# Decay arguments of a state-space mixer: from TensorE sums of bf16 parts to ScalarE sums of broadcast float32

## The chip, the cores and the metric

One core of a Trainium2 chip runs the whole program. The metric is the device time of one execution in microseconds, from the runs of the kernel and from one profiled execution. A difference of about 0.2% (4 us) is what a measurement of this kernel can tell from no change.

## The reference, cut to what matters

Four blocks follow one another on x of 2 x 512 x 512: a block-sparse linear layer, an int4 feed-forward layer, the mixer, and the same feed-forward layer again. Only the mixer changes. For each of 128 heads (H, 64 wide) and each chunk of 128 tokens:

```python
A_dt = A[None, None, :] * dt                  # A = -exp(A_log), dt = softplus(...)
A_cumsum = jnp.cumsum(Ac, axis=-1)            # within a chunk of 128 tokens
Lmat = jnp.exp(segment_sum(Ac))               # exp(cum[l] - cum[s]) for l >= s
Gm = jnp.einsum('bclhn,bcshn->bclsh', Cch, Bch)
M = Gm * jnp.transpose(Lmat, (0, 2, 3, 4, 1))
Y_diag = jnp.einsum('bclsh,bcshp->bclhp', M, xch)
decay_states = jnp.exp(A_cumsum[..., -1:] - A_cumsum)
decay_chunk = jnp.exp(segment_sum(A_last))    # A_last: the sums of whole chunks
```

## The kernel before, in words

The mixer works in steps. Step k (0 to 127) handles one pair of heads of one batch: batch k // 64, pair k % 64. A pair has 128 channels by 512 tokens (four chunks). Eight pairs share one group of B and C, so what is done by group falls at fixed places k % 8, called q here.

TensorE in step k, in program order: the projection of x for pair k+1 (L1013, 12 matmuls), `arguments(k)` (L1051), `outputs(k-1)` (L1094, L1100), the turn of x (L1065), the projection of z for pair k+1 (L1013), at q = 3 and 4 the projection of the next group's B or C, one tile of the output projection (L1113), and `states(k)` (L1078). At q = 5 `turn_b` and `gram` of the next group come in too. Projections and output tiles write three PSUM banks in turn, `RING`: each unit takes the bank of the third unit ahead of it, and `ring_free` waits until that one has been read. For an x that is the convolution on VectorE, for a z the silu on ScalarE (`silu_z`).

`arguments(k)` makes cum[l] - cum[s] of both heads in the PSUM tile `arg` (two banks, one pair at a time): the sum is kept in DRAM as three bf16 parts (`a_parts`), and the difference is a matmul over six rows, parts times one and minus one times parts. `exponent(k)` on ScalarE clamps it (Relu, L1284) and takes Exp (L1286) in place. `mask_em(k)` on VectorE (L1502) multiplies it with the masked gram tile into `em`, which `outputs(k)` reads in step k+1.

ScalarE in step k: `w_high` of the next x weights (the float32r copy, L1246), `wo_high`, `tap` of x for pair k+1 (L1258, first term of the convolution), `w_high` of the next z weights, `exponent(k)`, at q = 5 `copy_btok`, the silus of pair k+1 (L1263, L1268), `y_high` and `square` of pair k-1, `w_high` of a third unit if there is one (q = 2 and 3), and at q = 3 and 4 the tap of B or C, after C's also `activate_bc` (L1273). Exp and silu need different activation tables, so a step has two table loads.

GpSimd makes the low part of each weight tile (`w_low`, L1673) after `w_high`. SyncE issues every DMA in one in-order queue. Its pass k: the weights of `units_of(k + 1)` (x and z of pair k+2, and B or C as a third at q = 2 and 3), `load_args(k + 1)` (small parts, double-buffered), then `e_t` into `ce`, then output weights. There are only two raw weight buffers, so each weight load waits for `w_low` of the unit two places earlier: `sp.wait_ge(w_lo, u - NR + 1)`.

Ahead of step 0 stand the softplus of dt, the sums by chunk, their parts, and the decays of the states (`diff`, `dec_h`, transposed into `dec_q`, and `e_last`).

Of the kernel before, what the change touches and what calls it, by code (L numbers as in the profile page):

```python
# [5 lines left out]
P = 128  # L6
F32 = mybir.dt.float32
F32R = mybir.dt.float32r
BF16 = mybir.dt.bfloat16
# [28 lines left out]
K = B * JP  # L38
# [9 lines left out]
def build(nc, x_in, mask_t, wa_t, bias_a, w_in, conv_w, conv_b, dt_bias, a_log, d_res, norm_w, w_out,  # L48
          gu_w, gu_z, gu_s, dn_w, dn_z, dn_s, x_mid, e_t, a_parts, out):
    with ExitStack() as ctx:  # L50
# [655 lines left out]
        dt_q = sb("dt_q", [P, K, CPB, 2])  # L706
        dec_q = sb("dec_q", [P, K, OFFC, 2])
# [15 lines left out]
        a_left = sb("a_left", [P, 2, S], BF16)  # L723
        a_right = sb("a_right", [P, 2, S], BF16)
# [16 lines left out]
        cum = sbp("cum", [P, T, CS])  # L741
        diff = sbp("diff", [P, T, CS])
        dec_h = sbp("dec_h", [P, B * S])
        e_cum = sbp("e_cum", [P, B * S])
        rest = sbp("rest", [P, B * S])
        parts = sbp("parts", [P, 3, B * S], BF16)
        e_end = sbp("e_end", [P, T])
# [12 lines left out]
        adt_done, cum_mm, cum_done = sem("adt_done"), sem("cum_mm"), sem("cum_done")  # L760
        cum_exp = sem("cum_exp")
        dect_mm, decq_done = sem("dect_mm"), sem("decq_done")
        diag_done, last_mm, last_done = sem("diag_done"), sem("last_mm"), sem("last_done")
        parts_done, rest_done = sem("parts_done"), sem("rest_done")
        parts_stored, e_stored = sem("parts_stored"), sem("e_stored")

        wo_loaded = [sem(f"wo_loaded{j}") for j in range(2)]
        a_loaded = [sem(f"a_loaded{j}") for j in range(2)]
        e_loaded = [sem(f"e_loaded{j}") for j in range(2)]
        a_ones = sem("a_ones")  # L770
# [4 lines left out]
        arg_mm, arg_clamped, exp_done, em_done = sem("arg_mm"), sem("arg_clamped"), sem("exp_done"), sem("em_done")  # L775
# [96 lines left out]
        class Mixer:  # L872
# [57 lines left out]
            def sync(self, sp, tiles):  # L930
                def load_units(k):
                    for unit in units_of(k):
                        u = UNIT[unit]
                        if u < NR:
                            continue
                        sp.wait_ge(w_lo, u - NR + 1)
                        sp.dma_start(w_raw[:, u % NR], w_in[w_tile(unit)]).then_inc(w_loaded[u % NR], 16)

                def load_args(k):
                    b, h = batch(k), 2 * pair(k)  # L940
                    sp.wait_ge(a_ones, 4)
                    need(sp, arg_mm, k - 1)
                    for g in range(2):
                        at = 32 * g
                        sp.dma_start(a_right[at:at + 3, k % 2], a_parts[0:3, h + g, b * S:(b + 1) * S])\
                            .then_inc(a_loaded[k % 2], 16)
                        sp.dma_start(a_left[at + 3:at + 6, k % 2], a_parts[0:3, h + g, b * S:(b + 1) * S])\
                            .then_inc(a_loaded[k % 2], 16)
# [11 lines left out]
                load_units(-1)  # L960
                for i in range(3):
                    if i == 2:
                        load_units(1)
                    sp.wait_ge(parts_done, i + 1)
                    sp.dma_start(a_parts[i], parts[:, i]).then_inc(parts_stored, 16)
                sp.wait_ge(cum_exp, 3)
                sp.dma_start(e_t, e_cum[:]).then_inc(e_stored, 16)
                sp.wait_ge(parts_stored, 16 * 3)
                load_args(0)
                for k in range(K):  # L970
                    if k > 0:
                        load_units(k + 1)
                    if k + 1 < K:
                        load_args(k + 1)
                    if k == K - 1:
# [19 lines left out]
            def tensor(self, pe, n):  # L995
# [22 lines left out]
                def gram(n):  # L1018
                    pe.wait_ge(silu_bc, n + 1)
                    if n:  # L1020
                        k = QG * (n - 1) + 5
                        pe.wait_ge(xdec_done, k + 1)
                        pe.wait_ge(xdt_done, k + 1)
                    dst = gram_bank(n)
# [5 lines left out]
                def turn_b(n):  # L1030
# [3 lines left out]
                    else:  # L1034
                        pe.wait_ge(cum_done, B)
# [6 lines left out]
                def arguments(k):  # L1042
                    pe.wait_ge(a_loaded[k % 2], 64 * (k // 2 + 1))
                    need(pe, em_done, k)
                    if k == 0:
                        pe.wait_ge(btok_done, 1)
                        pe.wait_ge(decq_done, B)
                    for c in range(CPB):
                        for g in range(2):
                            rows = slice(32 * g, 32 * g + 6)  # L1050
                            mm = nc.tensor.matmul(ARG[:, g, c * CS:(c + 1) * CS],  # L1051
                                                  a_left[rows, k % 2, c * CS:(c + 1) * CS],
                                                  a_right[rows, k % 2, c * CS:(c + 1) * CS], start=True, stop=True)
                    mm.then_inc(arg_mm, 1)

                def turn_x(k):
                    pe.wait_ge(silu_x, k + 1)
                    if k == 0:
                        pe.wait_ge(decq_done, B)
# [9 lines left out]
                def states(k):  # L1069
                    pe.wait_ge(xdec_done, k + 1)  # L1070
                    pe.wait_ge(btok_done, k // QG + 1)
                    if k == 0:
                        pe.wait_ge(last_done, 1)
# [80 lines left out]
                def spread_last():  # L1154
                    pe.wait_ge(diag_done, B)
                    pe.wait_ge(adt_done, 2 * B)
                    nc.tensor.matmul(ST[:], ones[:], pre[:, 0:B * (OFFC - 1) * H], start=True, stop=True)\
                        .then_inc(last_mm, 1)

                def turn_dec():  # L1160
                    pe.wait_ge(rest_done, 4)
# [653 lines left out]
```

## Time and profile before

| what | value |
|---|---|
| median of 3 runs | 2142.29 us (2140.72 to 2142.93) |
| profiled execution | 2141.5 us, span of its trace 2139.8 us |
| TensorE matmul busy | 2102.7 us, 98% of the span |
| VectorE, ScalarE, GpSimd busy | 1689.4, 1401.8, 881.4 us |
| mean granted TensorE clock | 0.997 of full speed |
| DMA | 241.89 MB, 34.9% of 16 engines |

Read it from the chain of waits first: the engine that holds most of it sets the time, and the others matter only where they make that engine wait. A step that repeats is then read in the timeline, engine by engine.

### The profile page before, as it was taken

The page shows a single profiled execution, that of the slowest core. Times are in us where ns is not written, and L with a number is a line of the kernel's source. Part 1 is how long each engine was busy: PE and PEld are TensorE (multiplying, and loading weights), DVE is VectorE, ACT ScalarE, POOL GpSimd, SP SyncE. Part 2 cuts the span into 40 slices and gives each one's busy share as a digit, 9 for nine tenths or more (in the row PEclk, how much of TensorE's full clock was granted, in tenths as well). Part 3 has the DMA queues.
Part 4 walks back from the last instruction along what each step waited for, and adds up shares of the span by engine and source line. Part 5 has one row for each costly group of instructions (what it writes and reads, how often), then busy time and mean ns, then how long its engine had stood idle before and what let it go on. Part 6 is the DMA issues. An engine that isn't in the chain of part 4 may idle for free.

```text
span 2139.8 us, 37480 instructions
## 1 busy us (share of the span) xinstructions
PE 2102.7 (98%) x13386; PEld 1732.0 (81%) x13386; DVE 1689.4 (79%) x2679; ACT 1401.8 (66%) x1918; POOL 881.4 (41%) x622
## 2 busy tenths in 40 slices
PE   7999998999999999999999999999999999999999
PEld 6788876888888888888888888888888888878887
DVE  7555468988888888888898889898888888876554
ACT  5322277878787777777787877787777778752221
POOL 1222134545454545444454544544544545422221
PEclk9999998999999999999999999999999999999999
DMA  5543224233333333232333333342333233255441
GB/s 201 177 146 138 61 94 125 90 109 103 100 112 101 105 96 108 95 122 91 100 112 101 101 98 114 105 122 96 100 101 112 90 104 109 97 186 177 135 147 40
DMA packets 128644, 241.89 MB, mean 113 GB/s; under 512 B 14048, under 2 KB 48608, under 8 KB 128224
## 3 DMA queue, kind: packets, MB, share of 16 engines
q1 hardware_dynamic: 128480, 239.73, 34.9%
q8 instruction: 100, 1.64, 0.3%
q14 instruction: 64, 0.52, 0.1%
HBM read 234.17 MB, written 5.51 MB: 112 GB/s over the span
## 4 chain that ended last, share of the span: by engine, by line
PE 90%; DVE 3%; issue 3%; ACT 2%; DMA 1%; POOL 1%; SPq 0%; DVEq 0%; POOLq 0%; ACTq 0%
PE ring L1013 35%; PE ring L1113 16%; PE bank L412 6%; PE bank_e L412 6%; PE yt L1094 6%; PE st L1078 4%; PE yt L1100 4%; PE xt L1065 3%; PE bank_e L424 3%; PE bank L424 3%; PE arg L1051 2%; PE xt L1026 1%; PE bank L654 1%; DMA w_raw<-w_in 0%; DVE xr L304 0%
## 5 line engine op out<-in xcount | busy, mean ns | idle before, releaser
L1013 PE MATMUL ring<-m_lnt,w_sb 128*128 128x512 f32 x3456 | 859.9, 399 | 1.2 <-DVE xc L1440 1.2
L1013 PEld LDWEIGHTS ring<-m_lnt,w_sb 128*128 128x128 f32 x3456 | 633.0, 189 | 127.1 <-DVE xc L1440 1.5
L1673 POOL TENSOR_TENSOR w_sb<-w_raw,w_sb 128x512 fp32r<-128x512 f32 x288 | 401.7, 1400 | 177.3 <-ACT w_sb L1246 177.0
L1688 POOL TENSOR_TENSOR ysq<-ysq,y 128x512 f32<-128x512 f32 x126 | 162.8, 1292 | 652.8 <-ACT y L1290 652.8
L1113 PE MATMUL ring<-wo,ygs 128*128 128x512 f32 x1536 | 369.4, 390 | 2.0 <-issue 2.0
L1113 PEld LDWEIGHTS ring<-wo,ygs 128*128 128x128 f32 x1536 | 287.3, 188 | 63.2 <-issue 2.6
L1440 DVE SCALAR_TENSOR_TENSOR xc<-ring,cw,xc 128x511 f32<-128x511 f32 (+2 forms) x384 | 286.0, 745 | 23.0 <-ACT xc L1258 13.9
L1258 ACT ACTIVATE xc<-ring,cb,cw 128x512 f32<-128x512 f32 x128 | 99.2, 775 | 215.4 <-PE ring L1013 215.4
L1678 POOL TENSOR_TENSOR wo<-wo_raw,wo 128x512 fp32r<-128x512 f32 x128 | 214.0, 1672 | 0.0
L1246 ACT ACTIVATE w_sb<-w_raw 128x512 fp32r<-128x512 f32 x288 | 177.0, 619 | 26.8 <-DMA w_raw<-w_in 26.8
L1094 PE MATMUL yt<-em,x_dt 128*64 128x128 f32 x2048 | 183.7, 279 | 3.2 <-DVE state L1482 3.2
L1494 DVE TENSOR_TENSOR ce<-ce,bc 128x768 f32<-128x768 f32 x128 | 177.3, 1385 | 0.0
L328 POOL TENSOR_TENSOR f_gu<-f_gu_f,f_gu 128x1024 fp32r<-128x1024 f32 x28 | 67.3, 2402 | 255.7 <-ACT f_gu L351 255.7
L1476 DVE COPY state<-st 128x128 f32<-128x128 f32 x128 | 37.3, 292 | 168.9 <-PE st L1078 168.9
L1263 ACT ACT_TABLE_LOAD x127 | 162.9, 1283 | 2.3
L1286 ACT ACT_TABLE_LOAD x127 | 162.9, 1283 | 2.3
L1502 DVE TENSOR_TENSOR em<-arg,gt 128x1024 f32<-128x1024 f32 x128 | 155.8, 1217 | 2.5 <-ACT arg L1286 2.5
L412 PE MATMUL bank_e<-f_lnt,f_gu 128*128 128x512 f32 x672 | 154.3, 390 | 1.0 <-DVE f_lnt L141 1.0
L412 PE MATMUL bank<-f_lnt,f_gu 128*128 128x512 f32 x672 | 154.2, 390 | 0.6 <-DVE f_lnt L141 0.6
L1100 PE MATMUL yt<-ce,state 128*64 128x128 f32 x1536 | 149.3, 273 | 0.0
L412 PEld LDWEIGHTS bank_e<-f_lnt,f_gu 128*128 128x128 f32 x672 | 125.9, 188 | 27.4 <-DVE f_lnt L141 1.4
L412 PEld LDWEIGHTS bank<-f_lnt,f_gu 128*128 128x128 f32 x672 | 125.9, 188 | 27.1 <-DVE f_lnt L141 1.1
(203 smaller groups left out, 3159.2 us busy)
## 6 DMA issues: line engine op xcount, KB each, us to landing
w_raw<-w_in SPq DMA_DIRECT2D x288, 256.0 KB, 4.2
ce<-e_t SPq DMA_DIRECT2D x128, 384.0 KB, 4.1
wo_raw<-w_out SPq DMA_DIRECT2D x128, 256.0 KB, 4.4
f_gu_q<-gu_w SPq DMA_DIRECT2D x28, 512.0 KB, 3.7
f_gu_zr<-gu_z SPq DMA_DIRECT2D x28, 512.0 KB, 4.5
f_gu_sr<-gu_s SPq DMA_DIRECT2D x28, 512.0 KB, 5.3
f_dn_q<-dn_w SPq DMA_DIRECT2D x28, 256.0 KB, 3.5
f_dn_zr<-dn_z SPq DMA_DIRECT2D x28, 256.0 KB, 4.0
```

The costliest lines, as they stand in the source:

```text
L412: mm = nc.tensor.matmul(dst[half][:], gu[:, j, b, c:c + P], lnt[:, a, k, half * TOK:(half + 1) * TOK], start=(i == 0), stop=(i == 3 * KT - 1))
L1013: mm = nc.tensor.matmul(dst[:], w_sb[:, u % WR, wp, k * P:(k + 1) * P], lnt[:, xp, k, b * S:(b + 1) * S], start=(i == 0), stop=(i == 3 * K ...
L1094: mm = nc.tensor.matmul(YT[h * HD:(h + 1) * HD, c * CS:(c + 1) * CS], x_dt[:, at:at + HD], em[:, h, c * CS:(c + 1) * CS], start=True, stop ...
L1100: mm = nc.tensor.matmul(YT[h * HD:(h + 1) * HD, c * CS:(c + 1) * CS], state[:, c - 1, h * HD:(h + 1) * HD], ce[:, k % 2, h, (c - 1) * CS:c ...
L1113: mm = nc.tensor.matmul(dst[:], ygs[:, j % OR, yp, t * P:(t + 1) * P], wo[:, j % WOR, wp], start=(m == 0), stop=(m == 3 * HALF - 1))
L1246: nc.scalar.activation(w_sb[:, u % WR, 0], w_raw[:, u % NR], ACT.Copy).then_inc(w_hi, 1)
L1263: nc.scalar.activation(xc[:, k % 3], xc[:, k % 3], ACT.Silu).then_inc(silu_x, 1)
L1286: nc.scalar.activation(part, part, ACT.Exp, scale=-1.0).then_inc(exp_done, 1)
L1440: nc.vector.scalar_tensor_tensor(out=dst[:, d:S], in0=src[:, 0:S - d], scalar=cw[:, tile, j:j + 1], in1=dst[:, d:S], op0=ALU.mult, op1=ALU ...
L1494: nc.vector.tensor_tensor(ce[:, k % 2], ce[:, k % 2], c_off.rearrange("p (o t) -> p o t", o=1) .to_broadcast([P, 2, OFFC * CS]), ALU.mult) ...
L1673: nc.gpsimd.tensor_tensor(w_sb[:, u % WR, 1], w_raw[:, u % NR], w_sb[:, u % WR, 0].bitcast(F32), ALU.subtract).then_inc(w_lo, 1)
L1678: nc.gpsimd.tensor_tensor(wo[:, j % WOR, 1], wo_raw[:, j % 2], wo[:, j % WOR, 0].bitcast(F32), ALU.subtract).then_inc(wo_lo, 1)
```

## The change

The three bf16 parts, the matmuls over six rows and the tiles for them go. The sums are stored once in float32 (`c_t`) and each pair's two rows are loaded into all 128 partitions of one buffer, `cum_b`. `clamp` on ScalarE subtracts in its bias and clamps at once: Relu(cum_q - cum_b) by eight instructions, since the bias is one number per partition, head and chunk. `exponent` then reads `cum_b` and writes `arg`. Both run for pair k+1 in step k. The silus stand before the exponent in even steps and behind it in odd ones, so that a step has one table load.

```diff
+                def clamp(k):
+                    act.wait_ge(c_loaded, 16 * (k + 1))
...
+                    for h in range(2):
+                        for c in range(CPB):
+                            at = slice(c * CS, (c + 1) * CS)
+                            last = nc.scalar.activation(cum_b[:, h, at], cum_b[:, h, at], ACT.Relu, scale=-1.0,
+                                                        bias=cum_q[:, k, c, h:h + 1])
+                    last.then_inc(arg_clamped, 1)
+
                 def exponent(k):
-                    act.wait_ge(arg_mm, k + 1)
-                    part = ARG[:].rearrange("p h t -> p (h t)")
-                    nc.scalar.activation(part, part, ACT.Relu, scale=-1.0).then_inc(arg_clamped, 1)
                     act.wait_ge(arg_clamped, k + 1)
-                    nc.scalar.activation(part, part, ACT.Exp, scale=-1.0).then_inc(exp_done, 1)
+                    need(act, em_done, k)
...
+                    nc.scalar.activation(ARG[:], cum_b[:], ACT.Exp, scale=-1.0).then_inc(exp_done, 1)
```

ScalarE's step, then TensorE's, then the load of the sums on SyncE:

```diff
-                    if k < K:
-                        exponent(k)
+                    if k + 1 < K:
+                        clamp(k + 1)
                     for g in gram_in(k):
                         copy_btok(g)
-                    if k + 1 < K:
+                    if k + 1 < K and k % 2 == 0:
                         activate_x(k + 1)
                         activate_z(k + 1)
...
+                    if k + 1 < K:
+                        exponent(k + 1)
+                        if k % 2:
+                            activate_x(k + 1)
+                            activate_z(k + 1)
...
-                    if k < K:
-                        arguments(k)
                     if 1 <= k <= K:
                         outputs(k - 1)
...
                 def load_args(k):
                     b, h = batch(k), 2 * pair(k)
...
+                    need(sp, exp_done, k)
+                    sp.dma_start(cum_b[:], c_t[h:h + 2, b * S:(b + 1) * S]
+                                 .rearrange("(o h) t -> o h t", o=1).to_broadcast([P, 2, S])).then_inc(c_loaded, 16)
```

Ahead of step 0 the decays of the states come from matmuls with triangular or all-one matrices and an Exp, in place of `diff`, `rest` and the transposes: `cumulate_by_token` (two float32 matmuls 512 wide), `sum_later` (two, 384 wide) and `sum_chunks` (two, 256 wide). `dt_q` is copied earlier, x's third projection moves behind the first gram.

ScalarE in a step with q = 3. Before, with Exp (L1286) and both silus (L1263 x, L1268 z) ahead of `y_high` (L1296):

```order
L1284 ACTIVATE arg<-arg 128x1024 [waits arg_mm]
L1286 ACT_TABLE_LOAD
L1286 ACTIVATE arg<-arg 128x1024 [waits arg_clamped]
L1263 ACT_TABLE_LOAD
L1263 ACTIVATE xc<-xc 128x512 [waits conv_done]
L1268 ACTIVATE sz<-ring 128x512 [waits yg_lo,prj_mm]
L1296 ACTIVATE ygs<-sz 128x512 [waits yg_done]
L1290 ACTIVATE y<-y 128x512 [waits yg_done]
L1246 ACTIVATE w_sb<-w_raw 128x512 [waits prj_mm,w_loaded1]
L1258 ACTIVATE bc<-ring,cb,cw 128x512 [waits prj_mm]
```

The same step in the change, where the clamp is L1275, Exp L1285, the silus L1250 and L1255:

```order
L1275 ACTIVATE cum_b<-cum_b,cum_q 128x128 [waits c_loaded]
L1275 ACTIVATE cum_b<-cum_b,cum_q 128x128 x7
L1295 ACTIVATE ygs<-sz 128x512 [waits yg_done]
L1289 ACTIVATE y<-y 128x512 [waits yg_done]
L1233 ACTIVATE w_sb<-w_raw 128x512 [waits prj_mm,w_loaded1]
L1245 ACTIVATE bc<-ring,cb,cw 128x512 [waits prj_mm]
L1285 ACTIVATE arg<-cum_b 128x1024 [waits em_done,arg_clamped]
L1250 ACT_TABLE_LOAD
L1250 ACTIVATE xc<-xc 128x512 [waits conv_done]
L1255 ACTIVATE sz<-ring 128x512 [waits yg_lo,prj_mm]
```

Both silus have moved from the middle of the step to its end, behind the clamp, the tap of B and Exp.

SyncE's queue in the change, in the passes whose third weight load is B (first row) and C:

```order
L932 DMA w_raw<-w_in 128x512 [waits w_lo] x3
L937 DMA cum_b<-c_t 128x2x512 [waits exp_done]
L945 DMA ce<-e_t 128x2x384 [waits yt_mm]
L951 DMA wo_raw<-w_out 128x512
L932 DMA w_raw<-w_in 128x512 [waits w_lo] x3
L937 DMA cum_b<-c_t 128x2x512 [waits exp_done]
```

The load of `cum_b` stands where four small loads stood, behind all three weight loads, and now waits for the Exp that reads the same buffer.

## Rows read from the trace of the kernel before

**Rows 1.** The page: busy time by engine, and the chain by engine.
```profile
PE 2102.7 (98%) x13386; PEld 1732.0 (81%) x13386; DVE 1689.4 (79%) x2679; ACT 1401.8 (66%) x1918; POOL 881.4 (41%) x622
PE 90%; DVE 3%; issue 3%; ACT 2%; DMA 1%; POOL 1%; SPq 0%; DVEq 0%; POOLq 0%; ACTq 0%
```
**Rows 2.** Timeline of PE, one step: start us, us, operation, count.
```profile
1014.06 3.02 PE L1013 MATMUL ring<-m_lnt,w_sb 128*128 128x512 f32 x12
1017.00 0.40 PE L1051 MATMUL arg<-a_right,a_left 6*128 6x128 bf16 x8
1017.33 0.66 PE L1094 MATMUL yt<-em,x_dt 128*64 128x128 f32 x8
...
1019.42 2.99 PE L1013 MATMUL ring<-m_lnt,w_sb 128*128 128x512 f32 x12
1022.25 2.88 PE L1113 MATMUL ring<-wo,ygs 128*128 128x512 f32 x12
...
1025.56 3.02 PE L1013 MATMUL ring<-m_lnt,w_sb 128*128 128x512 f32 x12
```
**Rows 3.** Timeline of ACT, the same step.
```profile
1017.11 0.78 ACT L1258 ACTIVATE xc<-ring,cb,cw 128x512 f32<-128x512 f32 x1 [2.46 <-PE ring L1013]
1017.79 0.62 ACT L1246 ACTIVATE w_sb<-w_raw 128x512 fp32r<-128x512 f32 x1
1018.31 1.01 ACT L1284 ACTIVATE arg<-arg 128x1024 f32<-128x1024 f32 x1
1019.34 1.28 ACT L1286 ACT_TABLE_LOAD   x1
1020.63 1.01 ACT L1286 ACTIVATE arg<-arg 128x1024 f32<-128x1024 f32 x1
```
**Rows 4.** Timeline of DVE, the same step: the product `em`.
```profile
1023.38 1.22 DVE L1502 TENSOR_TENSOR em<-arg,gt 128x1024 f32<-128x1024 f32 x1
```
**Rows 5.** Timeline of ACT ahead of step 0: narrow and biased instructions.
```profile
291.22 0.58 ACT L135 ACTIVATE m_lnt<-xt 128x512 fp32r<-128x512 f32 x1
291.69 0.59 ACT L135 ACTIVATE m_lnt<-st 128x512 fp32r<-128x512 f32 x1
...
294.09 0.31 ACT L1327 ACTIVATE a_neg<-a_neg 128x128 f32<-128x128 f32 x1
294.30 0.61 ACT L1246 ACTIVATE w_sb<-w_raw 128x512 fp32r<-128x512 f32 x1
...
296.01 0.68 ACT L1334 ACTIVATE low<-arg,dtb_col 128x512 f32<-128x512 f32 x1
296.58 0.69 ACT L1335 ACTIVATE pre<-arg,dtb_col 128x512 f32<-128x512 f32 x1
```
**Rows 6.** Tile `ce` (384 KB, broadcast), then tile `w_raw` (256 KB): issue to landing.
```profile
DMA to landing us min/median/max: 3.3/4.1/5.4
DMA to landing us min/median/max: 2.5/4.2/6.0
```
**Rows 7.** Timelines of SP and POOL around the third weight load, q = 2.
```profile
1020.06 8.02 SPq L937 DMA_DIRECT2D w_raw<-w_in  x3
...
1026.43 1.30 POOL L1673 TENSOR_TENSOR w_sb<-w_raw,w_sb 128x512 fp32r<-128x512 f32 x1
```
**Rows 8.** Timelines of PE and ACT: starts of q = 4 and 5, silu of the C group.
```profile
1051.28 3.02 PE L1013 MATMUL ring<-m_lnt,w_sb 128*128 128x512 f32 x12
...
1065.50 3.02 PE L1013 MATMUL ring<-m_lnt,w_sb 128*128 128x512 f32 x12
...
1077.69 0.83 PE L1078 MATMUL st<-x_dec,b_tok 128*128 128x128 f32 x6
...
1069.35 1.06 ACT L1273 ACTIVATE bc<-bc 128x1024 f32<-128x1024 f32 x1 [4.96 <-DVE bc L1440]
```
**Rows 9.** Timeline of PE, first work of the program.
```profile
17.90 4.82 PE L654 MATMUL bank<-wa,f_lnt 128*128 128x512 f32 x12 [1.49 <-DVE wa L552]
```
**Rows 10.** One stretch: us, busy PE PEld DVE ACT POOL, PEclk, DMA share, GB/s.
```profile
300.00:340.00 40.00, 34.33 (x198) 26.85 (x197) 29.43 (x42) 31.44 (x42) 10.13 (x9) 0.87 0.33 109
```

More of the change, by code:

```diff
@@ L722, in build @@
         b_tok = sb("b_tok", [P, 2, OFFC * NS])
[L723 to L724 removed]
+        cum_b = sb("cum_b", [P, 2, S])
         scope_q, sbq = scope()
@@ L930, in sync, with load_units @@
             def sync(self, sp, tiles):
-                def load_units(k):
-                    for unit in units_of(k):
+                def load_units(units):
+                    for unit in units:
                         u = UNIT[unit]
@@ L940, in load_args, with load_decay @@
                     b, h = batch(k), 2 * pair(k)
[L941 to L948, printed above, removed]
+                    need(sp, exp_done, k)
+                    sp.dma_start(cum_b[:], c_t[h:h + 2, b * S:(b + 1) * S]
+                                 .rearrange("(o h) t -> o h t", o=1).to_broadcast([P, 2, S])).then_inc(c_loaded, 16)
+                def load_decay(k):
+                    b, h = batch(k), 2 * pair(k)
                     if k == 0:
@@ L1040, in turn_b @@
                     mm.then_inc(btok_mm, 1)
[L1042 to L1054, printed above, removed]
                 def turn_x(k):
@@ L1180, in tensor @@
                 cumulate()
+                for b in range(B):
+                    cumulate_by_token(b)
+                sum_later(0)
                 project(("x", 1))
+                sum_later(1)
+                sum_chunks()
                 project(("z", 1))
-                project(("x", 2))
                 gram(0)
                 turn_b(0)
-                turn_dec()
-                spread_last()
+                project(("x", 2))
                 for k in range(STEPS):
@@ L1342, in scalar @@
                 tap(("x", 0))
+                for b in range(B):
+                    act.wait_ge(cum_mm, b + 1)
+                    nc.scalar.activation(cum[:, b * S:(b + 1) * S], ARG[:, b], ACT.Copy).then_inc(cum_done, 1)
                 w_high(("z", 1))
@@ L1365, in scalar @@
-                nc.scalar.activation(e_cum[:], cum[:].rearrange("p c l -> p (c l)"), ACT.Exp).then_inc(cum_exp, 1)
+                    act.wait_ge(cumq_mm, b + 1)
+                    nc.scalar.activation(cum_q[:, b * JP:(b + 1) * JP],
+                                         (XT, ST)[b][:].rearrange("p (c j h) -> p j c h", c=CPB, h=2), ACT.Copy)\
+                        .then_inc(cumq_done, 1)
+                activate_x(0)
+                act.wait_ge(cum_done, B)
+                nc.scalar.activation(e_cum[:], cum[:], ACT.Exp).then_inc(cum_exp, 1)
@@ L1366, in scalar @@
+                for b in range(B):
+                    act.wait_ge(dec_mm, b + 1)
+                    part = (YT, ARG[:, 0])[b][:, 0:OFFC * H]
+                    nc.scalar.activation(part, part, ACT.Exp).then_inc(dec_exp, 1)
+                act.wait_ge(last_mm, 1)
+                nc.scalar.activation(e_last[:].rearrange("p b c h -> p (b c h)"), ARG[:, 1], ACT.Exp).then_inc(last_done, 1)
+                w_high(("x", 2))
                 tap(("x", 1))
                 copy_btok(0)
-                act.wait_ge(last_mm, 1)
@@ L1369, in scalar @@
-                nc.scalar.activation(e_last[:].rearrange("p b c h -> p (b c h)"), ST[:], ACT.Copy).then_inc(last_done, 1)
+                clamp(0)
+                exponent(0)
                 def factor_root(b):
@@ L1536, in vector @@
                     norm_low(dve, nm, t)
+                nc.vector.tensor_scalar(later[:], tri[:], -1.0, 1.0, ALU.mult, ALU.add).then_inc(later_done, 1)
                 conv(("b", 0))
```

159 lines of the change are left out of this document (64 added, 95 removed).

## The prediction

> **What bounds the kernel now.** I read the page first, then the chain, then one step in the timelines. Matmuls are busy 98% of the span and TensorE holds 90% of the chain [rows 1], so TensorE sets the time, and another engine matters only where it makes TensorE wait. One ordinary step shows it [rows 2]: x's projection starts at 1014.06 and the next step's at 1025.56, 11.50 us without a gap. ScalarE waits 2.46 us in it for that projection [rows 3]. Hence two questions: what TensorE is spared, and whether the work moved to ScalarE, the new load and the new order make it wait.
>
> **TensorE's part.** The eight small matmuls go in each step. From x's projection to the first output matmul it takes 1017.33 - 1014.06 = 3.27 us; a projection followed by other work takes 1022.25 - 1019.42 = 2.83 [rows 2]. So 0.44 us a step is saved (at least 0.33, from the first argument matmul to the next work), all on the path: 127 x 0.44 = 56 us. An ordinary step becomes 11.06 us; one with B or C has a projection more, 1065.50 - 1051.28 - 11.50 = 2.72 [rows 8], and becomes 13.78.
>
> **ScalarE's part.** It loses a Relu of 1.03 us and one table load of 1.29 [rows 3] and gains eight Relus of 128 columns with a bias. Nothing in the trace is both narrow and biased. A 128-column instruction gives way to the next after 294.30 - 294.09 = 0.21; a bias adds 0.57 - 0.47 = 0.10 to one of 512 columns read from PSUM [rows 5]. That makes 0.30, eight 2.4 us. Bounds: 8 x 0.21 = 1.7 and 8 x (0.31 + 0.10) = 3.3, no overlap. So ScalarE works about as long as before. A copy, silu or square of 512 columns gives way after 1018.31 - 1017.79 = 0.52, a tap after 0.68, Exp after 1.03 [rows 3]. What counts is the order.
>
> The table loads I take at their row, 1.29: Relu ends at 19.32, the load starts at 19.34 and Exp at 20.63 [rows 3], no gap at either side. The Trainium skill (ScalarE: Activation LUTs, What ACT_TABLE_LOAD costs) puts a drain of about 1.38 us beside each load; what that would make is a rival below.
>
> **The load.** `cum_b` is 512 KB in one buffer. A(k+1), the load for pair k+1, waits for Exp(k) and the clamp waits for it. `ce`, 384 KB in the same pattern, takes 3.3 to 5.4, median 4.1 [rows 6]; I take 4.3 for a load alone, 4.9 behind a weight load still under way, with 3.3 and 5.4 (4.1 and 5.8 behind weights) as bounds. The Trainium skill (Trainium Kernel Development and Optimization, Best Practices) asks for two buffers so that loads overlap work, which speaks against this buffer; here `ce` has two and no engine is listed as waiting for it, which agrees.
>
> **Ordinary steps hide it.** Times count from the start of x's projection. `em` ends 10.55 into a step (1023.38 + 1.22 - 1014.06 = 10.54 [rows 2, 4]), and Exp for the next pair waits for it. Odd step: Exp 10.55 to 11.6, that is 0.5 into the even step; table and silus to 2.85; load landed at about 4.9; after two copies, the tap (about 3.9 to 4.6) and a third copy the Relus run 5.2 to 7.6, silus to 8.6, `y_high` and `square` after the gate to 10.5, table to 11.8, Exp to 12.9 = 1.8 into the odd step. There the load lands at 6.2, Relus end at 8.6, copies at 10.4, Exp at 11.6 again. TensorE wants x's silu at 4.5: no wait. SyncE's other waits (`ce` for the outputs, 4.6 into a step) come ahead of it; GpSimd and VectorE keep their work.
>
> **Steps q = 2, 3 and 4 do not.** In SyncE's queue A stands behind three weight loads, and the third waits for `w_low` of x, which follows ScalarE's first copy of that step. Before, three loads stretched over 8.02 us [rows 7] and nobody missed what stood behind.
> - q = 2: Exp ended at 0.5, silus at 2.85, the copy at 3.4, `w_low` (1.30, [rows 7]) at 4.8; weights are issued, then A at 5.3; lands 10.2; Relus 12.6; silus 13.6; two copies 14.7; copy of B 15.2; table 16.5; Exp 17.5, 6.4 into step q = 3.
> - q = 3: copy 7.0, `w_low` 8.3, A issued 8.8, lands 13.7, Relus 16.1, two copies 17.1, copy of C 17.6, tap of B 18.3, Exp 19.3, table 20.6, silu of x 21.1, silu of z 21.6.
> - With B in the ring, the next x takes the bank of that z. TensorE would start it at 13.78 and waits till 21.7: **7.9 us** in each of 15 groups.
>
> **Step q = 5.** The C silu ends 1069.35 + 1.06 - 1065.50 = 4.9 into it [rows 8]. Exp now stands behind it: 7.2 with its table load. The load lands at 11.6, Relus 14.0, `copy_btok` behind them 14.4. The state matmuls wait for that copy; they would start at 1077.69 - 1065.50 - 0.44 = 11.75. **2.75 us** more in each group.
>
> **The clock.** After the first 10 us, in which TensorE had nothing, 12 matmuls took 4.82, in the steps 3.02 [rows 2, 9]. In [rows 10], with TensorE waiting for 5.7 of 40 us, the granted clock is 0.87 on average: a part of it ran at 1.2 GHz, not 2.4. A wait of 7.9 should do the same: 4.82 - 3.02 = 1.8 for the projection after it and some for the matmuls behind, 2.3 us a group, 35 in all. Bounds: none, and twice that if step q = 5 falls too.
>
> **Ahead of step 0.** TensorE gets two float32 matmuls of 512, two of 384 and two of 256 columns (about 4.6 us at some 1.0 for 512), and loses six turns and one wide matmul (1.7). VectorE and GpSimd lose work, fewer steps wait for each other, and TensorE waited 5.7 us there [rows 10]. I take zero, with 8 us to either side. The 64 MB more of transfers find engines 35% busy; they are in the bounds of the load.
>
> **Sum.** 2141.5 - 56 + 15 x (7.9 + 2.75) + 35 = 2280 us; the median shown lies 0.8 above the profiled run, so **2281**.
>
> **Rivals.**
> - *The loads come in time: faster.* If A reached its buffer early enough at q = 2 and 3 (short transfers, Relus nearer 0.1 us), only the 56 us would show: 2142 - 56 = 2086. For it: ScalarE has slack in ordinary steps, and the 127 savings are certain. Against: the wait at q = 3 is 7.9; a load counts in it twice, the Relus twice. Even both at their low bound (4.1, 1.7) leave 7.9 - 1.6 - 1.4 = 4.9, and 2.75 - 1.0 - 0.7 = 1.05 at q = 5; 15 x 5.95 = 89 is more than 56 (2175). It decides at 3.7 us a group.
> - *The same waits, clock kept: slower.* No row has a wait this long amid dense work; the 10 us of the start are longer, the waits of [rows 10] were many. 2281 - 35 = 2246.
> - *Every pair of steps is bound by the loop of load, Relus and Exp.* Two loads, two sets of Relus, silus 1.0, four copies 2.1, one table 1.3, two Exps 2.1: 19.9 of the 22.1 us that two steps last, so it does not bind. With 5.4 and 3.3 it would take 23.9, 0.9 a step over 96 steps: about 2281 + 86 = 2367.
> - *A table load costs more than its row.* If ScalarE drained for 1.38 us at each load, the loads ahead of Exp at q = 2, ahead of silu at q = 3 and ahead of Exp at q = 5 would add 4.1 a group: 2343. Rows 3 show no such gap. The Trainium skill (the section named above) states that drain.
> - The change could also fail to run a pair ahead. It does so only while Exp waits for nothing but `em`; that is the forecast itself.
>
> **How the numbers follow.** Chances: the forecast 0.55, clock kept 0.18, loads in time 0.13, the loop 0.09, the drain 0.05. Low end: Relus and loads low, TensorE at full clock, 2175, with a few us for the start: 2170. High end: the loop's 2367, a little inside it, 2360. That leaves out most of "in time" and half of "the loop". Faster by over 0.2% needs the first rival: 0.12. Within 0.2%: 0.02. Slower: 0.86.
>
> **What would show it.** Right: TensorE waits on ScalarE's silu of z some 15 times, 6 to 9 us each, and in the state matmuls of q = 5 on `b_tok`, 2 to 4 each; step period 11.06 elsewhere; ScalarE waits on `cum_b` in most steps; eight Relus at 0.30 from start to start; half as many table loads in the steps; granted clock dips 15 times. Wrong: no wait of x's projection on a silu, the weight load issued earlier at q = 2, or waits at every step. The prediction fails first if the ring's wait at q = 4 is under 3 us.

## The result, and the profile after

| | before | after |
|---|---|---|
| median | 2141.7 us (2140.72 to 2142.93, 4 runs) | 2300.97 us (2297.87 to 2303.03, 4 runs) |
| ratio to before, 95% interval | | 1.0742 (1.0724 to 1.0761) |
| span of the profiled execution | 2139.8 us | 2301.3 us |
| mean granted TensorE clock | 0.997 | 0.965 |
| table loads of ScalarE in the mixer's steps | 254 | 131 |

The kernel became 7.4% slower: 159 us by the medians, 161.5 by the spans. The page of the profile after, its engines, its chain and the new load:

```profile
PE 2114.0 (92%) x12366; PEld 1733.5 (75%) x12366; DVE 1614.7 (70%) x2676; ACT 1429.7 (62%) x2690; POOL 848.8 (37%) x616
...
PE 56%; ACT 15%; DVE 9%; DMA 8%; issue 8%; POOL 3%; SPq 0%; ACTq 0%; DVEq 0%; POOLq 0%
...
cum_b<-c_t SPq DMA_DIRECT2D x128, 512.0 KB, 3.8
```

Beside [rows 1], TensorE fell from 98% of the span to 92% and from 90% of the chain to 56%. It shows 1020 matmuls fewer and is yet busy 11 us longer; the mean granted clock fell from 0.997 to 0.965. ScalarE, VectorE and the load are on the chain now. TensorE's waits after (where, for whom, us in all, times, longest):

```profile
PE ring L1007 <- ACT sz L1255: 102.2, 14, 8.8
PE ring L1095 <- POOL wo L1675: 32.1, 15, 2.1
...
PE st L1060 <- DVE x_dec L1468: 11.1, 6, 6.2
PE st L1060 <- ACT b_tok L1265: 3.7, 7, 0.7
```

An ordinary step of TensorE after (start, us, what):

```profile
1173.36 3.02 PE L1007 MATMUL ring<-m_lnt,w_sb 128*128 128x512 f32 x12
1176.31 0.66 PE L1076 MATMUL yt<-em,x_dt 128*64 128x128 f32 x8
...
1177.99 0.66 PE L1047 MATMUL xt<-ident,xc 128*128 128x128 f32 x4
...
1184.56 3.02 PE L1007 MATMUL ring<-m_lnt,w_sb 128*128 128x512 f32 x12
```

It takes 1184.56 - 1173.36 = 11.20 us without a gap, against 11.50 [rows 2]. From x's projection to the first output matmul it is now 2.95 us, not the 2.83 that was forecast. The long steps of the same group (the row at 1218.14 is x's projection of q = 3, that at 1239.37 of q = 4, that at 1254.91 of q = 5; in brackets the wait ahead of a row):

```profile
1218.14 3.02 PE L1007 MATMUL ring<-m_lnt,w_sb 128*128 128x512 f32 x12
1222.76 0.66 PE L1047 MATMUL xt<-ident,xc 128*128 128x128 f32 x4
1223.17 5.73 PE L1007 MATMUL ring<-m_lnt,w_sb 128*128 128x512 f32 x24
...
1239.37 4.64 PE L1007 MATMUL ring<-m_lnt,w_sb 128*128 128x512 f32 x12 [7.08 <-ACT sz L1255]
1245.62 0.66 PE L1047 MATMUL xt<-ident,xc 128*128 128x128 f32 x4
...
1254.91 3.02 PE L1007 MATMUL ring<-m_lnt,w_sb 128*128 128x512 f32 x12
...
1265.43 4.33 PE L1095 MATMUL ring<-wo,ygs 128*128 128x512 f32 x12 [2.14 <-POOL wo L1675]
...
1271.34 3.00 PE L1007 MATMUL ring<-m_lnt,w_sb 128*128 128x512 f32 x12
```

Where the time lies is best told by the turn of x (`xt<-ident,xc`), once in each of the 128 steps. "First 7" is the sum of the first seven distances from one turn to the next. The last three columns are means over the 14 groups behind the first. "Ordinary" is the median of the other 78 distances (their mean is 11.52 before and 11.23 after):

```
us                   first 7   ordinary   q=3 to 4   q=4 to 5   q=5 to 6
before                  81.4      11.50      14.22      14.22      12.76
after                   92.8      11.19      23.64      13.91      15.93
```

That is the whole difference: +11.4 at the start (q = 3 to 5 of the first group are in it), 78 ordinary distances at -0.30 by their means, and 14 times +9.42, -0.31 and +3.17; the rest, +1.3, lies nearly all behind the last step. What TensorE is spared is worth some 33 us, as the next section shows by itself; 195 are lost to waits and to the clock behind them.

### The profile page after: what moved, and what is told of

The parts are those of the page before. It is cut to its first block, busy times and chain, and to the rows that moved or that the text cites. A ratio compares the mean times of both kernels' runs of the same rounds, so it can differ in the third digit from the quotient of the medians.

```text
span 2301.3 us, 35693 instructions
## 1 busy us (share of the span) xinstructions
PE 2114.0 (92%) x12366; PEld 1733.5 (75%) x12366; DVE 1614.7 (70%) x2676; ACT 1429.7 (62%) x2690; POOL 848.8 (37%) x616
## 4 chain that ended last, share of the span: by engine, by line
PE 56%; ACT 15%; DVE 9%; DMA 8%; issue 8%; POOL 3%; SPq 0%; ACTq 0%; DVEq 0%; POOLq 0%
PE ring L1007 20%; PE ring L1095 9%; DMA cum_b<-c_t 8%; PE bank L411 6%; PE bank_e L411 6%; ACT cum_b L1275 4%; PE bank_e L423 3%; PE yt L1076 3%; PE bank L423 3%; PE st L1060 2%; POOL w_sb L1670 2%; PE yt L1082 2%; ACT L1250 2%; ACT L1285 2%; ACT w_sb L1233 2%
## 5 line engine op out<-in xcount | busy, mean ns | idle before, releaser
L1007 PE MATMUL ring<-m_lnt,w_sb 128*128 128x512 f32 x3456 | 888.7, 409 | 105.1 <-ACT sz L1255 102.2
L1007 PEld LDWEIGHTS ring<-m_lnt,w_sb 128*128 128x128 f32 x3456 | 650.9, 194 | 242.5 <-ACT sz L1255 104.8
L1275 ACT ACTIVATE cum_b<-cum_b,cum_q 128x128 f32<-128x128 f32 x1024 | 313.4, 390 | 211.8 <-DMA cum_b<-c_t 211.8
L1095 PE MATMUL ring<-wo,ygs 128*128 128x512 f32 x1536 | 382.7, 399 | 35.3 <-POOL wo L1675 32.1
L1095 PEld LDWEIGHTS ring<-wo,ygs 128*128 128x128 f32 x1536 | 293.6, 192 | 104.0 <-issue 40.3
L1685 POOL TENSOR_TENSOR ysq<-ysq,y 128x512 f32<-128x512 f32 x126 | 161.5, 1282 | 545.0 <-ACT y L1289 545.0
L1675 POOL TENSOR_TENSOR wo<-wo_raw,wo 128x512 fp32r<-128x512 f32 x128 | 187.2, 1463 | 4.4 <-ACT wo L1301 4.4
L1076 PEld LDWEIGHTS yt<-em,x_dt 128*64 128x64 f32 x2048 | 119.0, 137 | 51.0 <-issue 51.0
L1500 DVE TENSOR_TENSOR ce<-ce,bc 128x768 f32<-128x768 f32 x128 | 150.5, 1176 | 0.0
```

Of the source, the lines that this page charges most:

```text
L1007: mm = nc.tensor.matmul(dst[:], w_sb[:, u % WR, wp, k * P:(k + 1) * P], lnt[:, xp, k, b * S:(b + 1) * S], start=(i == 0), stop=(i == 3 * K ...
L1076: mm = nc.tensor.matmul(YT[h * HD:(h + 1) * HD, c * CS:(c + 1) * CS], x_dt[:, at:at + HD], em[:, h, c * CS:(c + 1) * CS], start=True, stop ...
L1095: mm = nc.tensor.matmul(dst[:], ygs[:, j % OR, yp, t * P:(t + 1) * P], wo[:, j % WOR, wp], start=(m == 0), stop=(m == 3 * HALF - 1))
L1275: last = nc.scalar.activation(cum_b[:, h, at], cum_b[:, h, at], ACT.Relu, scale=-1.0, bias=cum_q[:, k, c, h:h + 1])
L1675: nc.gpsimd.tensor_tensor(wo[:, j % WOR, 1], wo_raw[:, j % 2], wo[:, j % WOR, 0].bitcast(F32), ALU.subtract).then_inc(wo_lo, 1)
L1685: nc.gpsimd.tensor_tensor(part, part, y[:, k % 2], ALU.add).then_inc(ysq_done, 1)
```

## Experiments

The next table holds the distances of every run, so that the sections can be short. A median comes from all of a kernel's runs, the distances from its one profiled execution. "One", "two" and "three moves" name the edits in the order in which they come below.

```
us                                  median   first 7   ordinary   q=3 to 4   q=4 to 5   q=5 to 6
before                              2142        81.4      11.50      14.22      14.22      12.76
arguments left out (of before)      2109.5      79.0      11.19      13.91      13.92      12.74
after                               2301.0      92.8      11.19      23.64      13.91      15.93
one Relu for eight                  2256.4      85.8      11.19      21.51      13.91      15.09
silus ahead at q=3                  2263.5      96.3      11.19      20.86      13.90      15.55
load ahead                          2191.6      87.6      11.19      15.86      13.91      16.08
both                                2167.9      90.8      11.19      13.98      14.14      15.84
Exp ahead of C's tap and silu alone 2268.2      91.5      11.19      24.17      13.91      12.74
all three                           2144.2      92.5      11.19      13.92      14.00      13.69
all three, tap in step 0            2147.3      94.7      11.19      13.93      14.04      14.31
all three, Exp between tap and silu 2131.5      92.0      11.19      14.00      14.15      13.41
```

### What TensorE is spared

The kernel before, without the argument matmuls (eight in each step) and the loads of their operands behind step 0. Exp then waits for `em` where it had waited for the matmuls:

```diff
                 def load_args(k):
...
+                    if k == 0:
+                        sp.wait_ge(a_ones, 4)
...
-                    if k < K:
+                    if k == 0:
                         arguments(k)
...
                 def exponent(k):
-                    act.wait_ge(arg_mm, k + 1)
+                    act.wait_ge(arg_mm, 1)
+                    need(act, em_done, k)
```

> The kernel before, with the four argument matmuls and the loads of their operands left out of every step after the first (the exponentials of later steps then start from what lies in PSUM, so the chunk factors are not the reference's). It measures what the removal alone is worth to TensorE, with nothing put in its place. Theory, from the ordinary step of the changed kernel (11.19 to 11.20 us against 11.50): the step ends 0.31 us earlier, 127 steps give 39 us, so about 2102 us and an ordinary step of 11.19. Rival, the prediction's term: 0.44 us a step, 56 us, so about 2086 us and a step of 11.06; the changed kernel's step would then be held 0.13 us longer by something else that it added.

Measured: 2109.49 us (2107.59 to 2109.84), ratio 0.9847 (0.9832 to 0.9863), 32.7 us less than before. Its ordinary step:

```profile
1014.29 0.66 PE L1065 MATMUL xt<-ident,xc 128*128 128x128 f32 x4
...
1020.86 3.02 PE L1013 MATMUL ring<-m_lnt,w_sb 128*128 128x512 f32 x12
1023.80 0.66 PE L1094 MATMUL yt<-em,x_dt 128*64 128x128 f32 x8
...
1025.48 0.66 PE L1065 MATMUL xt<-ident,xc 128*128 128x128 f32 x4
```

The step is 11.19 us and the projection takes 2.94 to the first output matmul, as after the change, though nothing that the change added stands in this kernel. So nothing that the change added holds the ordinary step; the output matmuls simply start 0.1 us later behind a projection (2.94) than an output tile does (2.83, [rows 2]). The step from q = 5 to 6 keeps its 12.76 but for 0.02. The step is the one that the theory had; the total, 33 us, is less than the 39 and 56 of both theories: 0.3 in most steps and nothing in those at q = 5.

### The silus ahead of the exponential at q = 3

In the change the silus stand behind Exp in every odd step, q = 3 among them, where z's silu frees the bank for x's projection of q = 4.

```diff
-                    if k + 1 < K and k % 2 == 0:
+                    if k + 1 < K and (k % 2 == 0 or bc_units(k)):
                         activate_x(k + 1)
                         activate_z(k + 1)
...
-                        if k % 2:
+                        if k % 2 and not bc_units(k):
```

> Both silus of q = 3 stand ahead of Exp again (as in even steps), at the price of one more table load there. Theory (the z silu that stands last at q = 3 holds the ring's bank): the load of cum_b is still late, so the silus come right behind the Relus, 15.5 us into the step, plus a table load and both silus: 17.8 instead of 21.2. TensorE's wait at q = 4 falls from 7.1 to about 3.7, 15 times: 50 us less, 2250, up to 25 more off if the clock then stays up. Rival (ScalarE has too much work in every step, order matters little): the added table load makes it no faster, 2300 to 2320.

Measured: 2263.46 us (2261.0 to 2265.21), ratio 1.0567 (1.0549 to 1.0584). The ring wait fell from 102.2 to 59.8 us, 3.0 less a group, and stayed in all 14: with the silus first, they still stand behind the Relus, and these behind the load. The gain is 37.5 us and not 50, since the theory had 3.4 for 15 groups and the first seven distances grew by 3.5. The rival (2300 or more) falls: the place of the silus matters more than one table load more. What the change itself shows of that chain, on ScalarE and on SyncE's queue (L932 issues weights, L937 `cum_b`; a row's length there includes its waits for free buffers):

```profile
1206.14 1.03 ACT L1285 ACTIVATE arg<-cum_b 128x1024 f32<-128x1024 f32 x1
...
1216.42 2.45 ACT L1275 ACTIVATE cum_b<-cum_b,cum_q 128x128 f32<-128x128 f32 x8 [4.60 <-DMA cum_b<-c_t]
...
1222.75 1.03 ACT L1285 ACTIVATE arg<-cum_b 128x1024 f32<-128x1024 f32 x1
...
1231.31 2.44 ACT L1275 ACTIVATE cum_b<-cum_b,cum_q 128x128 f32<-128x128 f32 x8 [3.88 <-DMA cum_b<-c_t]
...
1235.88 1.01 ACT L1285 ACTIVATE arg<-cum_b 128x1024 f32<-128x1024 f32 x1
1236.91 1.28 ACT L1250 ACT_TABLE_LOAD   x1
...
1238.74 0.58 ACT L1255 ACTIVATE sz<-ring 128x512 f32<-128x512 f32 x1
```

```profile
1201.42 10.68 SPq L932 DMA_DIRECT2D w_raw<-w_in  x3
1212.14 0.43 SPq L937 DMA_DIRECT2D cum_b<-c_t  x1
...
1214.27 11.78 SPq L932 DMA_DIRECT2D w_raw<-w_in  x3
1226.10 0.43 SPq L937 DMA_DIRECT2D cum_b<-c_t  x1
```

Exp had read the buffer at 1207.17, but the load goes out at 1212.14, behind three weight loads; likewise 1223.78 and 1226.10. That is 5.0 and 2.3 us of queue.

### The load ahead of the third weight load

```diff
                     if k > 0:
-                        load_units(units_of(k + 1))
+                        load_units(units_of(k + 1)[0:2])
                     if k + 1 < K:
                         load_args(k + 1)
+                    if k > 0:
+                        load_units(units_of(k + 1)[2:])
+                    if k + 1 < K:
                         load_decay(k + 1)
```

> SyncE issues the load of cum_b ahead of the third weight load instead of behind it; nothing else changes. Theory: at q = 2 the load starts when the Exp before it ends and lands some 5 us earlier, Exp for q = 3 ends 2.0 us into that step instead of 5.8, the silu of z at about 15.0 instead of 21.2, so TensorE's wait at q = 4 falls from 7.1 to about 1.1 and the clock stays up there: 15 x 7.6 = 114 less, 2187. The waits at q = 5 stay. Rival (steps are bound by the loop of load, Relus, Exp anyway): under 30 us less, above 2270.

Measured: 2191.63 us (2187.51 to 2192.68), ratio 1.0225 (1.0207 to 1.0242): 109 us of the loss gone by the order of one queue. The two main waits are now:

```profile
PE ring L1098 <- POOL wo L1678: 32.3, 15, 2.3
PE ring L1010 <- ACT sz L1258: 19.4, 14, 3.0
```

The theory holds (2187 said). 1.4 us a group are left at the ring. In 11 of the 14 groups the wait is 0.9 to 1.2 us, and the distance of 15.0 to 15.4 is 13.91, the wait and 0.2 more: so short a wait costs no clock. The other three waited 2.8 to 3.0 us and took 16.9, 18.6 and 20.0. By itself the move in the queue takes 83 us of the ring wait away and the place of the silus 42; together that is more than the 102 there were, so the two overlap, and the queue counts for more.

### Both moves

> The two edits together. Theory: the last 1.1 us of the ring's wait go too, against one table load in slack time: 15 to 20 us less than with the load ahead alone, about 2170. What is left over 2142 - 39 is then the wait and the clock of q = 5, 15 x 4.0 = 60, and a few us at the start. Rival (each edit removes the same wait): the same time as with the load ahead alone.

Measured: 2167.9 us (2163.44 to 2169.97), ratio 1.0117 (1.0101 to 1.0134). The ring wait is gone (13.98 us from q = 3 to 4, 13.91 without any wait), as expected, and the gain over the load ahead alone, 24 us, speaks against the rival of the same time. What remains is q = 5 and the start.

### Step q = 5

The wait there is for `wo`, not for `b_tok`. In the change, ScalarE and GpSimd:

```profile
1258.76 1.06 ACT L1260 ACTIVATE bc<-bc 128x1024 f32<-128x1024 f32 x1 [6.18 <-DVE bc L1447]
1259.84 1.28 ACT L1285 ACT_TABLE_LOAD   x1
1261.13 1.03 ACT L1285 ACTIVATE arg<-cum_b 128x1024 f32<-128x1024 f32 x1
...
1262.62 0.61 ACT L1301 ACTIVATE wo<-wo_raw 128x512 fp32r<-128x512 f32 x1
...
1266.76 2.45 ACT L1275 ACTIVATE cum_b<-cum_b,cum_q 128x128 f32<-128x128 f32 x8 [2.35 <-DMA cum_b<-c_t]
1269.12 0.47 ACT L1265 ACTIVATE b_tok<-st 128x384 f32<-128x384 f32 x1
```

```profile
1264.02 1.27 POOL L1675 TENSOR_TENSOR wo<-wo_raw,wo 128x512 fp32r<-128x512 f32 x1
```

The first of a set of four output tiles needs the last output weights, whose low half GpSimd ends at 1265.29; TensorE starts at 1265.43. The high half stands behind C's silu, and now also behind a table load and Exp, 2.3 us. Exp moved ahead of them, first with nothing else moved:

```diff
+                    early_exp = k + 1 < K and k % QG == 4 and len(bc_units(k)) > 0
+                    if early_exp:
+                        exponent(k + 1)
                     for unit in bc_units(k):
                         tap(unit)
                         if unit[0] == "c":
                             activate_bc(unit[1])
                     if k + 1 < K:
-                        exponent(k + 1)
+                        if not early_exp:
+                            exponent(k + 1)
```

> The change, with the exponential placed ahead of the C group's tap and silu in step q=4 and nothing else moved. Theory (the wait at the first output tile of step q=5 is for the low half of a w_out tile, which POOL makes from a high half that ScalarE makes behind tap, silu of C, table load and exponential): that wait of 2.1 us goes with the dip of TensorE's clock behind it (some 1.5 us), 3.6 us a group of 15, about 54 us less, so about 2247 us, and step q=4's ring wait stays. Rival (the wait is made elsewhere, by the load of the sums or by the copy of B's tokens, which this does not bring forward): at most 0.5 us a group, 2293 us or more.

Measured: 2268.21 us (2265.39 to 2272.72), ratio 1.0595 (1.0579 to 1.0611). The distance from q = 5 to 6 fell from 15.93 to 12.74 and the wait on `wo` left the list, so the place is shown. The gain was 33 us by the medians, not 54, and 38 by the profiled spans: 14 x 3.19 = 45, less 14 x 0.53 = 7 that came back at the ring (24.17 against 23.64). The expectation had 3.6 a group for 15 groups; the dip of the clock does not follow every such wait. The rival (at most 0.5 a group) falls.

With the two other moves as well:

> Both edits, and at q = 4 Exp stands ahead of the tap and the silu of C. Theory: the wait at q = 5 (the output projection on the low part of the output weights, made behind the ScalarE work that Exp delays) goes with its dip of the clock: 60 us less than with both edits alone, about 2110, faster than the kernel before by 30 (ratio 0.985). Rival (q = 5 waits because three copies and the eight Relus are too much for that step): at most 15 us less, 2155 or more.

Measured: 2144.21 us (2134.79 to 2150.89, 10 runs), ratio 1.0013 (0.9999 to 1.0026): no different from before. That is 24 us less than with both moves: not the 60 of the theory, and more than the rival's 15. By the profiled spans it is 30: 14 x (15.84 - 12.74) = 43 were to be had at q = 5, of which C's silu, now behind Exp, takes 13 back (13.69 against 12.74), and the start 2. Against the run with the arguments left out, 13.5 us are lost in the first seven distances and 13 at C's silu; the two together eat nearly all of the 33 that the removal is worth. The waits:

```profile
PE st L1037 <- ACT bc L1263: 15.2, 8, 6.9
PE st L1063 <- DVE x_dec L1475: 11.0, 5, 6.2
```

### How much ScalarE's length matters

This kernel leaves out the subtraction, so that the eight Relus become one of the same columns:

```diff
-                    for h in range(2):
-                        for c in range(CPB):
-                            at = slice(c * CS, (c + 1) * CS)
-                            last = nc.scalar.activation(cum_b[:, h, at], cum_b[:, h, at], ACT.Relu, scale=-1.0,
-                                                        bias=cum_q[:, k, c, h:h + 1])
+                    last = nc.scalar.activation(cum_b[:], cum_b[:], ACT.Relu, scale=-1.0)
```

> The change, with one Relu of 1024 columns without the bias in place of the eight of 128 columns (the subtraction of the position's own sum is left out, so the decay factors are not the reference's). It shortens ScalarE's path by about 2.36 - 1.0 = 1.36 us in every step. Theory (the time is lost only where ScalarE and the load stand ahead of TensorE, that is in the three long steps of a group): the ring wait of step q=4 falls by about 1.4 us for each of the two late Relu groups in that chain and the wait at the first output tile by up to 1.4, so 2.7 to 4 us a group, 40 to 60 us in all, about 2250 us, with an ordinary step unchanged at 11.2. Rival (ScalarE's length bounds ordinary steps as well): 127 x 1.36 = 170 us less, about 2130 us.

Measured: 2256.35 us (2253.97 to 2258.97), ratio 1.0537 (1.052 to 1.0553), 45 us less, with an ordinary step still of 11.19. ScalarE's length is not what bounds an ordinary step; 1.36 us less of work a step is worth 2.1 + 0.8 a group and 7 at the start. The rival falls.

### The start

The version with all three moves, and the tap of pair 2 one step earlier:

```diff
-                    if 0 < k < K - 1:
+                    if 1 < k < K - 1:
                         tap(("x", k + 1))
+                    if k == 0:
+                        tap(("x", 2))
```

> The change with all three moves (load of the sums ahead of the third weight load, silus ahead of the exponential in step q=3, exponential ahead of the C group in step q=4), and the tap of x of pair 2 moved from step 1, where it stands behind the exponential of pair 1, to step 0 ahead of the Relus. Theory: the start's wait of 6.2 us for x_dec goes, with the half clock behind it, 6 to 9 us less than without the tap's move (2144 us), so 2135 to 2138 us, just faster than the kernel before (2142). Rival: the steps after the start absorb it, because ScalarE is late there anyway, and the time stays at 2144 within 2 us.

Measured: 2147.25 us (2144.14 to 2159.1, 11 runs), ratio 1.0031 (1.0018 to 1.0044). The wait of 6.2 us for `x_dec` went, but the first seven distances sum to 94.7, not less than 92.5: another wait took its place (2.6 us for a low weight half), and TensorE was no earlier in step 5. The theory falls; the rival holds in its reason, though the time is 3 us above the 2144 that it gave within 2. ScalarE still waits 3.8 and 3.7 us for the loads of `cum_b` of pairs 1 and 2; that these make the loss at the start is likely, but no run shows it.

### A version that beats both

The moves of the load and of the silus stay as they are; at q = 4, Exp stands between C's tap and C's silu (against the change):

```diff
                     for unit in bc_units(k):
                         tap(unit)
+                    if k + 1 < K:
+                        exponent(k + 1)
+                    for unit in bc_units(k):
                         if unit[0] == "c":
                             activate_bc(unit[1])
                     if k + 1 < K:
-                        exponent(k + 1)
```

> As the version with all three moves, but in step q=4 the exponential stands between the tap of C and the silu of C, not ahead of both. With it ahead of both (2144 us), the silu of C waits for VectorE's taps of C, and TensorE for that silu (15.2 us in all, 6.9 of it in the first group); step q=5 then takes 13.4 us against 12.8 without a wait. Table load and exponential, 2.3 us, are as long as VectorE's three taps of C (2.32 us), so they fit beside them. Theory: the silu of C starts about 1 us earlier, step q=5 takes 12.8 us, 0.6 us less for 14 groups and 1 to 2 us at the start: about 2134 us, faster than the kernel before (2142) by some 0.4%. Rival: the exponential, now 0.8 us later, lets the load of the next sums start later, the Relus of q=5 wait for it, and the w_out tile behind them is late again: 2145 us or more.

Measured: 2131.54 us (2131.25 to 2135.14, 5 runs), ratio 0.9948 (0.9935 to 0.9962): faster than the kernel before by 0.5%. ScalarE at q = 4:

```profile
1265.38 0.77 ACT L1248 ACTIVATE bc<-ring,cb,cw 128x512 f32<-128x512 f32 x1
1266.17 1.28 ACT L1288 ACT_TABLE_LOAD   x1
1267.46 1.03 ACT L1288 ACTIVATE arg<-cum_b 128x1024 f32<-128x1024 f32 x1
1268.51 1.28 ACT L1263 ACT_TABLE_LOAD   x1
1269.80 1.06 ACT L1263 ACTIVATE bc<-bc 128x1024 f32<-128x1024 f32 x1
```

Table load and Exp fit where VectorE does C's other taps. The mechanism held in part: six of 14 groups have no wait left from q = 5 to 6 (12.7 to 12.8), the others take 13.6 to 14.0, and TensorE still waits 13.7 us in all for C's silu. The profiled spans are only 2 us apart (2135.4 and 2133.4), since the profiled execution of the version with Exp ahead of both was among its fastest; the runs of that version spread over 16 us, those of this one over 4. How much of the 12.7 us between the medians comes from this move in the steps, one profile of each does not show.

## Why the prediction was right

It said 2281 us, slower, by a wait for the silu of z at q = 4 and a second wait at q = 5; it is 2301, slower, with the first wait where and as long as it was said, and the second at another product. Term by term:

| term | predicted | measured |
|---|---|---|
| TensorE's saving | 127 x 0.44 = 56 | 33 |
| ring wait | 15 x 7.9 = 118 | 102 in 14 groups (the first group's is in the start) |
| wait at q = 5 | 15 x 2.75 = 41, on `b_tok` | 30 on `wo` and 3 on `b_tok` in 14 groups |
| clock | 15 x 2.3 = 35 | 34 at q = 4, 11 at q = 5, in 14 groups |
| ahead of step 0 | 0, 8 to either side | 0 (x's first turn at 322.3 us, before at 322.5) |
| first group | 13, in the three terms above | 14 in the first seven distances, by other waits |

The sum came within 20 us because its errors partly cancel: in the 14 groups the two waits were said 14 us too long and the clock 13 us too cheap, and the saving was said 23 us too large.

- **TensorE's saving was mis-sized.** "A projection followed by other work takes 2.83" held for an output tile as the other work, not for the output matmuls that really follow: there it is 2.94 to 2.95, with or without the change. The lower bound the text gave, 0.33, was the better value: an ordinary step gives back 0.31 and lasts 11.19 us, not 11.06. And the 14 steps at q = 5 save nothing. This is the largest error, 23 us.
- **ScalarE's part held.** The eight Relus take 2.37 from start to start of what follows (1216.42 to 1218.79 in the profile after), 0.30 each. ScalarE waits on `cum_b` in 80 of 128 steps, and no ordinary step of TensorE shows it.
- **The ring wait held.** Against the start of q = 3 (1218.14): load issued at 8.0 (said 8.8), Relus from 13.2 to 15.5 (13.7 to 16.1), Exp 17.7 to 18.7 (said to end at 19.3), silu of z at 21.2 (21.6), the wait 7.1 (7.9). The runs with one and with both moves show the two causes that the chain had: the third weight load ahead of `cum_b` in SyncE's queue, and the silus behind Exp.
- **Step q = 5: near in size, wrong in mechanism.** The chain to the copy ran as said: against the start of q = 5 (1254.91), C's silu ends at 4.9, Exp at 7.2, the Relus start at 11.9 (said 11.6) and `b_tok` ends at 14.7 (said 14.4). But "the state matmuls wait for that copy" was not it: they start at 1270.75, 15.8 into this step, and wait 0.7 at most in any. TensorE had already waited 2.1 us ahead of them, for output weights that hang on the same late Exp. That is the step of the prediction that failed. It followed `copy_btok` and left out `wo_high`, which stands earlier in ScalarE's order and was on time in every row of before. The run with Exp moved alone shows it. That both products come late by the same Exp is why the size is near: in four groups whose clock stayed up the two waits add up to 2.7 to 2.8 us. That it met the forecast 2.75 is in part luck.
- **The clock held at q = 4.** The 4.82 us of [rows 9] had no granted clock beside it and was read as the lower level by its length alone; the 4.64 after the ring wait stands beside a granted 0.50. At q = 4 the projection after the wait took 4.64 instead of 3.02; the distance of 23.64 less 13.92 and less the mean wait of 7.3 leaves 2.4 a group (said 2.3), of which 0.2 follow such a wait even at full clock. That q = 5 would dip as well was in the bounds only; it did in seven of 14 groups, 1.5 us each.
- **The first group: right in size by luck.** Its share of the sum was 13 us; the first seven distances are 13.8 longer than in the run with the arguments left out. But the forecast wait for z's silu is not among them (there are 14 of them, not 15): TensorE waits 6.2 us for `x_dec` in step 1, 4.7 for x's silu at q = 4 and 2.1 for `wo`. The text did not follow the first loads of `cum_b`, for which ScalarE waits in steps 0 and 1.

Of the rivals, "loads in time" is excluded by the waits, "the loop binds" by the steps of 11.20, "clock kept" by the clock rows below. The drain of 1.38 us beside a table load, which the Trainium skill (ScalarE: Activation LUTs, What ACT_TABLE_LOAD costs) states, is in no row: Exp ends at 1236.89, the load starts at 1236.91, ends at 1238.19, and x's silu starts at 1238.20. That half of the table loads went brought nothing in ordinary steps: the step is 11.19 us with two (arguments left out) as with one (after). The run with one Relu shows the price of ScalarE's time where it matters: about 3 us a group for 1.36 us a step.

Not tried: two buffers for `cum_b`, which would let the load start a step earlier. What that would give back, no run shows.

## What to carry to other kernels

A load put into an in-order queue waits with everything ahead of it, so place it by what it needs, not by where its step stands: here one move in the queue made up for 109 of the 159 us. When work moves to an engine that has slack on average, follow every product behind it in that engine's order at the steps with extra work, not only the product moved, and put an instruction that needs a change of activation table where another engine's work covers it. What removing work from the bounding engine is worth is read from the time between the two neighbours that will really meet.

## What the runs showed of the hardware

TensorE's granted clock fell also after waits of only 1.8 to 3 us, and not each time. Each row is 2 us; the columns are its length, busy time of matmuls, weight loads, VectorE, ScalarE and GpSimd, the granted clock, and the DMA's share and GB/s. After the ring wait of 7.08 us, in the profile after:

```profile
1238.00:1240.00 2.00, 0.63 (x2) 0.53 (x3) 2.00 (x4) 1.99 (x5) 0.08 (x1) 0.50 0.80 254
1240.00:1242.00 2.00, 2.00 (x6) 1.61 (x5) 0.40 (x1) 0.36 (x1) 2.00 (x2) 0.50 0.36 139
```

and after the wait of 2.14 us that ended at 1265.43:

```profile
1266.00:1268.00 2.00, 2.00 (x8) 1.58 (x7) 1.97 (x5) 1.24 (x5) 0.53 (x1) 0.69 1.02 337
1268.00:1270.00 2.00, 2.00 (x8) 1.61 (x7) 1.89 (x2) 2.00 (x7) 0.00 (x0) 0.50 0.45 169
```

Both times the clock stood at the lower of its two levels, 1.2 GHz (0.50), for some microseconds of full work. In the run with one Relu the same wait came in the same place and the clock stayed:

```profile
1238.70 2.97 PE L1095 MATMUL ring<-wo,ygs 128*128 128x512 f32 x12 [2.15 <-POOL wo L1671]
```

```profile
1240.00:1242.00 2.00, 2.00 (x13) 1.73 (x12) 1.97 (x4) 1.44 (x2) 0.00 (x0) 1.00 0.95 343
```

There 12 of 14 distances from q = 5 to 6 were 14.8 to 15.2 (12.74 and the wait) and two 16.4; after the change they lie between 14.9 and 16.4. A wait of 2.1 us therefore costs TensorE between 2.1 and 3.7 us here. After the change seven of the 14 dipped. In the run with the load ahead alone, waits of nearly the same length at the ring were followed by projections at full or at half clock (first two rows), and with all three moves the clock fell after a wait of 1.77 us (granted 0.51 from 1268 to 1270 us; the projection that follows takes 4.57):

```profile
1591.22 3.01 PE L1010 MATMUL ring<-m_lnt,w_sb 128*128 128x512 f32 x12 [2.77 <-ACT sz L1258]
1382.76 5.49 PE L1010 MATMUL ring<-m_lnt,w_sb 128*128 128x512 f32 x12 [3.04 <-ACT sz L1258]
```

```profile
1267.13 0.55 PE L1037 MATMUL st<-ident,bc 128*128 128x128 f32 x3 [1.77 <-ACT bc L1263]
```

After the 11 ring waits of 0.9 to 1.2 us in the run with the load ahead it never fell. Why it dips in one group and not in the next, these runs do not settle.
